# A graph layer with attention over 100,000 edges: earlier dst rows, two row tiles for the edge products, pieces of a second branch spread differently

## The reference, cut to what matters

```
xn  = layernorm(x)                                    # 6250 nodes x 256
q, k, v = xn @ Wq.T + bq, ...                         # 8 heads of 32
e   = edge_attr @ We.T                                # 100,000 edges, 64 -> 256
alpha = sum((q[dst]) * (k[src] + e)) / sqrt(32)       # per edge and head
w   = softmax of alpha over the edges of one dst
gnn = segment_sum((v[src] + e) * w, dst) + xn @ Wskip.T + bskip
mix = linear attention over all nodes, Wo, layernorm, relu FFN 256-1024-256, layernorm
x   = x + gnn + mix
out = x + mixture of 8 experts (three 256x256 layers each, all experts, softmax gates) of layernorm(x)
```

## Time and profile before

| | us |
|---|---|
| three runs | 3732.03, 3732.52, 3723.98 (median 3732.03) |
| profiled execution | 3703.33 |
| its span | 3701.4 |

### The profile page before, as it was taken

How to read it: one execution, slowest core, us unless ns; L and a number is a source line. 1 busy time by engine, 2 the same in 40 slices (tenths; PEclk the granted TensorE clock), 3 DMA queues, 4 the chain that set the end, 5 groups by cost and what they waited for, 6 DMA issues and landing times.

```text
span 3701.4 us, 72350 instructions
## 1 busy us (share of the span) xinstructions
PE 3241.8 (88%) x17312; PEld 2525.9 (68%) x17312; DVE 2927.2 (79%) x6394; ACT 1719.3 (46%) x4685; POOL 1259.3 (34%) x1313
## 2 busy tenths in 40 slices
PE   4998899999999899999999177777768999999999
PEld 3775566666666666666666145555558999999999
DVE  6776898898888888888888888888856666666665
ACT  1222333333333333333333156666646777777776
POOL 1223666666666666666664021111100000000000
PEclk9998999999999999999999599999979999999999
DMA  7336988898888988888888256666610000000000
GB/s 177 116 115 172 243 250 238 234 249 242 243 245 238 245 237 244 244 246 239 245 238 222 91 173 207 206 207 206 207 60 12 12 17 11 17 11 17 11 17 9
DMA packets 520911, 593.54 MB, mean 160 GB/s; under 512 B 187937, under 2 KB 396979, under 8 KB 520319
## 3 DMA queue, kind: packets, MB, share of 16 engines
q1 hardware_dynamic: 312408, 351.02, 32.7%
q0 software_dynamic: 201888, 232.77, 24.1%
q10 hardware_dynamic: 6409, 7.46, 0.6%
HBM read 426.91 MB, written 163.17 MB: 159 GB/s over the span
## 4 chain that ended last, share of the span: by engine, by line
PE 52%; DVE 18%; issue 13%; SPq 5%; DMA 3%; DVEq 3%; ACT 3%; ACTq 2%; another core or an unknown queue 0%
PE psum L635 10%; PE psum L637 10%; PE psum L636 10%; PE psum L713 6%; PE psum L697 5%; DMA region_s<-ab_d 3%; DVE weights L1373 3%; DVE part L1387 3%; PE psum L849 3%; PE psum L770 2%; DVE region_s L1572 2%; DVE region_x L1560 1%; ACTq L1088 1%; ACT region_s L1083 1%; DVEq L1563 1%
## 5 line engine op out<-in xcount | busy, mean ns | idle before, releaser
L600 POOL DMA_INDIRECT weights<-kv_tab,idx x450 | 547.7, 1217 | 351.9 <-ACT idx L1006 192.1
L1012 ACT ACTIVATE weights<-psum,region_s 125x250 f32<-125x250 f32 x450 | 211.7, 471 | 951.2 <-PE psum L713 524.6
L697 PE MATMUL psum<-we,weights 64*125 64x256 f32 x1800 | 578.4, 428 | 6.5 <-issue 3.4
L849 PE MATMUL psum<-region_s 125*125 125x264 f32 x1800 | 453.9, 401 | 128.8 <-DVE region_s L1572 128.8
L713 PE MATMUL psum<-region_x,weights 125*125 x1800 | 546.9, 429 | 0.0
L1129 ACT ACTIVATE region_s<-psum,bns 128x250 f32<-128x250 f32 x800 | 403.4, 555 | 287.2 <-PE psum L637 287.2
L1622 DVE TENSOR_TENSOR parts_h<-region_s,parts_h 128x500 fp32r<-128x500 f32 x400 | 269.9, 679 | 312.4 <-ACT parts_h L1133 283.1
L849 PEld LDWEIGHTS psum<-region_s 125*125 125x125 f32 x1800 | 304.6, 188 | 277.9 <-issue 152.7
L713 PEld LDWEIGHTS psum<-region_x,weights 125*125 125x125 f32 x1800 | 320.3, 198 | 190.2 <-issue 159.6
L600 POOL DMA_INDIRECT kv_more<-kv_tab,idx x300 | 364.2, 1214 | 142.6 <-issue 102.0
L697 PEld LDWEIGHTS psum<-we,weights 64*125 64x125 f32 x1800 | 291.2, 190 | 163.2 <-issue 148.0
(11 more groups left out here) (246 smaller groups left out, 7628.2 us busy)
## 6 DMA issues: line engine op xcount, KB each, us to landing
region_s<-ve_d SPq DMA_DIRECT2D x450, 256.0 KB, 2.9
ve_d<-weights SPq DMA_DIRECT2D x225, 256.0 KB
ve_d<-kv_more SPq DMA_DIRECT2D x150, 256.0 KB
weights<-in_attr_t SPq DMA_DIRECT2D x450, 62.5 KB
ve_d<-region_r SPq DMA_DIRECT2D x75, 256.0 KB
kv_tab<-region_s SPq DMA_DIRECT2D x50, 224.0 KB
region_s<-ab_d SPq DMA_DIRECT2D x450, 1.0 KB
weights<-kv_tab,idx POOLq DMA_INDIRECT x450
```

What stands on the lines that cost most here:

```text
L600: nc.gpsimd.indirect_dma_start(kg[r][0:T, w, :], None, kv_tab, bass.IndirectOffsetOnAxis(idx[:, r, w:w + 1], 0)).then_inc(gathered[r], 16)
L697: last = mm(psum[0:T, s % 2, w * D:(w + 1) * D], att_b[:, s % RP, w * T:(w + 1) * T], we[:, :], start=True, stop=True)
L849: last = mm(bank, hot[:, s, w, :], pv[:, s, w, 0:PV], start=(w == 0), stop=(w == 1))
```

## The change

The dst rows of a step are loaded three steps sooner, first thing in SP's step. The edge attributes of a pair go to 128 partitions (tile 0 in rows 0 to 63, tile 1 in rows 64 to 127, rows of 500 bytes), the weights `we` are loaded twice, and the two edge products of a step run one after the other on the two row halves, each into a bank of its own, 0 and 1; so product k waits for add k-1. `spread`'s operands move to rows 0 to 63, and it follows both products. The query product runs one step ahead of the edge product. The pieces of the branch get other steps, the last four products of `down` in the next block, and `up`'s banks change. DVE's register loads go behind the add, in D behind the first product. In D the one-hots of step 0 come from DVE, of 1, 3 and 5 from ACT, of 2 and 4 from POOL by two compares each.

```diff
+AHEAD = 3
...
-BY_DVE = {0: 1, 3: 2}
-BY_ACT = {1: 1, 2: 2, 4: 3, 5: 4}
+BY_DVE = {0: 1}
+BY_ACT = {1: 1, 3: 2, 5: 3}
+BY_POOL = {2: 1, 4: 2}
...
-we = sb("we", [ED, D])
+we = sb("we", [2 * ED, D])
...
-ab_b = carve(8200, RP * E2 // 2).bitcast(BF16).rearrange("p (r n) -> p r n", r=RP)[64:128]
-coef = weights[64:128, 1600:1600 + 64].bitcast(BF16)[:, 0:T]
+ab_b = carve(8200, RP * E2 // 2).bitcast(BF16).rearrange("p (r n) -> p r n", r=RP)[0:64]
+coef = weights[0:64, 1600:1600 + 64].bitcast(BF16)[:, 0:T]
...
-att_b = weights[0:ED, 0:RP * E2].rearrange("p (r t) -> p r t", r=RP)
+att_b = weights[:, 0:RP * T].rearrange("p (r t) -> p r t", r=RP)
...
-hot_dve, hot_act = sem("hot_dve"), sem("hot_act")
+hot_dve, hot_act, hot_pool = sem("hot_dve"), sem("hot_act"), sem("hot_pool")
...
-CONST_A, CONST_B = 16 * 7, 16 * 9
+CONST_A, CONST_B = 16 * 7, 16 * 10
...
-    sp.dma_start(we[:, :], a["w_e"]).then_inc(c_b, 16)
+    for w in range(2):
+        sp.dma_start(we[w * ED:(w + 1) * ED, :], a["w_e"]).then_inc(c_b, 16)
...
+    ab_regs = [sp.alloc_register(f"sp_ab{s}") for s in range(SU)]
     def load_ab(k, s, reg):
...
+    sp.load(ab_regs, walk[0:1, 0, 0:SU])
+    for s in range(AHEAD):
+        load_ab(s, s, ab_regs[s])
...
     def b_body(b, u):
...
+                sp.load(ab_regs, walk[0:1, 0, bass.ds(k + AHEAD, SU)])
+            if k + AHEAD < STEPS:
+                load_ab(k + AHEAD, (s + AHEAD) % SB, ab_regs[s % SU])
...
-            sp.dma_start(att_b[:, s % RP, :], a["attr_t"][:, bass.ds(i * E2, E2)]).then_inc(att_in[s % RP], 16)
-            load_ab(k, s, regs[s % SU])
+            sp.dma_start(att_b[:, s % RP, :], a["attr_t"][:, bass.ds(i * E2, E2)].rearrange("p (w t) -> w p t", w=2)).then_inc(att_in[s % RP], 16)
...
+    order = Order(pool, pool_o)
     def d_body(it):
-        for s in BY_ACT:
+        for s in range(SU):
+            if s in BY_DVE:
+                continue
...
-            nc.gpsimd.tensor_tensor(place_in[:, s, :], pv[:, s, :, D + H], jb_all[:, bass.ds(k, 1)].broadcast_to((T, 2)),
-                                    ALU.subtract).then_inc(place_ready, 1)
+            placed = nc.gpsimd.tensor_tensor(place_in[:, s, :], pv[:, s, :, D + H], jb_all[:, bass.ds(k, 1)].broadcast_to((T, 2)),
+                                             ALU.subtract)
+            if s in BY_ACT:
+                placed.then_inc(place_ready, 1)
+            else:
+                order(placed)
+                for w in range(2):
+                    compared = nc.gpsimd.tensor_scalar(hot[:, s, w, :], iota[:, :], place_in[:, s, w:w + 1], None, ALU.is_equal)
+                compared.then_inc(hot_pool, 1)
+        order.reset()
...
-    def eproj(k, s, turn_of, w):
-        if w == 0:
-            pe.wait_ge(att_in[s % RP], turn_of * 16)
-            wait(pe, kv_added, k - 1)
-        last = mm(psum[0:T, s % 2, w * D:(w + 1) * D], att_b[:, s % RP, w * T:(w + 1) * T], we[:, :], start=True, stop=True)
-        if w == 1:
-            last.then_inc(e_done, 1)
+    def eproj(k, s, turn_of):
+        pe.wait_ge(att_in[s % RP], turn_of * 16)
+        wait(pe, kv_added, k)
+        for w in range(2):
+            half = slice(w * ED, (w + 1) * ED)
+            last = mm(psum[0:T, w, 0:D], att_b[half, s % RP, :], we[half, :], start=True, stop=True)
+        last.then_inc(e_done, 1)
     def spread(k, s, turn_of):
...
-            if n == 4 and not (isinstance(b, int) and b == NB - 1):
-                pe.wait_ge(m_an, b + 2)
...
-                pe.wait_ge(m_hr, b * 4 + pair - 1)
+                pe.wait_ge(m_hr, b * 4 + pair)
...
-                last = mm(psum[:, 5 + pair % 2, o * BN:(o + 1) * BN], wm1[:, c, n * 128:(n + 1) * 128], mx1t[:, c, :],
+                last = mm(psum[:, 5 if pair == 0 else 6, o * BN:(o + 1) * BN], wm1[:, c, n * 128:(n + 1) * 128], mx1t[:, c, :],
...
-    mix_at = {2: ("q", 0), 3: ("q", 1), 7: ("attend",), 10: ("turn",), 11: ("out", 0), 12: ("out", 1)}
-    late_at = {1: ("turn1",), 3: ("up", 0), 4: ("up", 1), 5: ("up", 2), 6: ("up", 3), 10: ("up", 4), 11: ("up", 5),
-               12: ("up", 6), 13: ("up", 7), 14: ("down", 0, 3), 15: ("down", 3, 7), 16: ("down", 7, 11), 17: ("down", 11, 16)}
+    mix_at = {2: ("q", 0), 3: ("q", 1), 8: ("attend",), 11: ("turn",), 12: ("out", 0), 13: ("out", 1)}
+    late_at = {1: ("turn1",), 4: ("up", 0), 5: ("up", 1), 6: ("up", 2), 7: ("up", 3), 9: ("up", 4), 10: ("up", 5),
+               11: ("up", 6), 12: ("up", 7), 14: ("down", 0, 3), 15: ("down", 3, 6), 16: ("down", 6, 9), 17: ("down", 9, 12)}
+    last_at = {0: ("down", 12, 14), 1: ("down", 14, 16)}
     def b_body(b, u):
...
-                pe.load(regs, walk[0:1, 1, bass.ds(k, SU)])
-            some = s >= LAGQ or not (isinstance(b, int) and b == 0)
-            if some:
-                eproj(k - LAGQ, (s - LAGQ) % SB, b * (SB // RP) + (s - LAGQ) // RP + 1, 0)
+                pe.load(regs, walk[0:1, 1, bass.ds(k + 1, SU)])
+            if s >= LAGQ or not (isinstance(b, int) and b == 0):
+                eproj(k - LAGQ, (s - LAGQ) % SB, b * (SB // RP) + (s - LAGQ) // RP + 1)
...
-            if some:
-                eproj(k - LAGQ, (s - LAGQ) % SB, b * (SB // RP) + (s - LAGQ) // RP + 1, 1)
-                qprod(k - LAGQ, (s - LAGQ) % SB, regs[s % SU])
+            if s >= LAGQ - 1 or not (isinstance(b, int) and b == 0):
+                qprod(k - LAGQ + 1, (s - LAGQ + 1) % SB, regs[s % SU])
+            if s in last_at and not (isinstance(b, int) and b < 2):
+                mix(b - 2, u, last_at[s])
...
-    pe.load(regs, walk[0:1, 1, STEPS:STEPS + SU])
+    pe.load(regs, walk[0:1, 1, STEPS + 1:STEPS + 1 + SU])
...
-        eproj(STEPS - LAGQ + s, SB - LAGQ + s, (STEPS - LAGQ + s) // RP + 1, 0)
+        eproj(STEPS - LAGQ + s, SB - LAGQ + s, (STEPS - LAGQ + s) // RP + 1)
...
-        eproj(STEPS - LAGQ + s, SB - LAGQ + s, (STEPS - LAGQ + s) // RP + 1, 1)
-        qprod(STEPS - LAGQ + s, SB - LAGQ + s, regs[s])
-    for g in late_at.values():
+        if s < LAGQ - 1:
+            qprod(STEPS - LAGQ + 1 + s, SB - LAGQ + 1 + s, regs[s])
+        if s in last_at:
+            mix(NB - 2, 1, last_at[s])
+    for g in (*late_at.values(), *last_at.values()):
...
     def sums(k, s, it):
...
+        elif s in BY_POOL:
+            pe.wait_ge(hot_pool, it * len(BY_POOL) + BY_POOL[s])
...
-                last = fn(mh[:, n, :], psum[:, 5 + pair % 2, o * BN:(o + 1) * BN], ACT.Relu,
+                last = fn(mh[:, n, :], psum[:, 5 if pair == 0 else 6, o * BN:(o + 1) * BN], ACT.Relu,
...
-    mix_at, late_at = {1: "phi", 8: "turn", 17: "turn1"}, {2: 0, 4: 1, 9: 2, 11: 3}
+    mix_at, late_at = {1: "phi", 9: "turn", 17: "turn1"}, {3: 0, 5: 1, 8: 2, 10: 3}
     def b_body(b, u):
...
-        tt(rows4, rows4, psum[0:T, s % 2, :].rearrange("p (w d) -> p w d", w=2).unsqueeze(2).broadcast_to((T, 2, 2, D)),
+        tt(rows4, rows4, psum[0:T, 0:2, 0:D].unsqueeze(2).broadcast_to((T, 2, 2, D)),
...
     def multiply(k, s):
...
-    mix_at = {0: "phi", 3: "attend", 8: "sum1", 9: "stats1", 10: "root", 11: "root2", 12: "norm1", 13: "gain1"}
+    mix_at = {0: "phi", 4: "attend", 8: "sum1", 9: "stats1", 10: "root", 11: "root2", 12: "norm1", 13: "gain1"}
...
-    last_at = {1: "root2", 4: "norm2", 5: "gain2", 6: "add2"}
+    last_at = {1: "root2", 3: "norm2", 5: "gain2", 6: "add2"}
     def b_body(b, u):
...
-            if s % SU == 0:
-                dve.load(regs, walk[0:1, 2, bass.ds(k, SU)])
...
+            if s % SU == 0:
+                dve.load(regs, walk[0:1, 2, bass.ds(k, SU)])
...
     def d_body(it):
-        dve.load(regs, walk[0:1, 1, bass.ds(it * SU + LAGQ - LAG, SU)])
...
+            if s == 0:
+                dve.load(regs, walk[0:1, 1, bass.ds(it * SU + LAGQ - LAG, SU)])
```

## The result

| | us |
|---|---|
| before, beside it | 3732.28 (3723.98 to 3742.75) |
| after | 3815.53 (3809.42 to 3822.16, 4 runs) |
| ratio | 1.0222, 95% interval 1.0191 to 1.0253 |
| forecast | 3667, range 3580 to 3745 |

What follows compares the result with a forecast made beforehand. DVE was taken to bound both stages, with PE nearly full in the edge stage. Edge stage -16 us and segment sums -49 made -65, from the median 3732.0 to 3667 us, range 3580 to 3745.

Steps and rivals of the forecast that it cites:

- the one on SP: SP's queue: store and attribute load behind the earlier dst rows are needed over 15 us later; cost 0, bound +150.
- Register load behind the add: Edge stage: load hidden by the add at steps 0 and 6, outlasting it at step 12; -41 us (-79 to 0).
- `out` 1 too late: Edge stage: moved to PE step 13, `out` makes DVE wait before `sum1`, 2.5 us a block; +63 us (0 to +76).
- PE's waits: Edge stage: of some 60 us of DVE waits for PE and remote, 38 go and 22 stay; -38 us.
- Segment sums: Segment-sum stage: one one-hot leaving DVE -29, load moved -50, DVE delayed by POOL compares +30; -49 us together.
- the lock's +30: Segment-sum stage: POOL compares and DVE products block each other, 0.1 us a compare; +30 us, bounds 0 and +138.
- Row tiles overlap: Edge stage, PE: both edge products run side by side, 0.85 us to the first query pass, empty step 1.9 us.
- B: Rival, chance 0.13: low clock in PE steps 11 to 13 doubles DVE's wait for `out` in twelve blocks; 3780 us.
- A: Rival, chance 0.16: PE ahead everywhere, `out` in time, no wait for PE stays in the edge stage; -180, 3552 us.
- C: Rival, chance 0.05: in the segment sums all 300 compares block DVE whole; +138 instead of +30, 3775 us.
- D: Rival, chance 0.06: in the edge stage row tiles don't overlap, edge products stay in sequence; +13, 3680 us.
- listed as "right": Edge products starting together; 2.5 us idle a block before `sum1`; no dst-row wait; segment sums near 524 us; POOL compares stretched.

Runs made afterwards that it cites:

- e2: The changed kernel with each pair's attributes laid out as 128 plain DRAM rows, so the load is two-dimensional: 3569.1 us, ratio 0.9600.
- e9: e2 with DVE's edge-stage register load back at the head of steps 0, 6 and 12: 3645.9 us, ratio 0.9810.
- e7: e2 with `out` 1 a step earlier, at PE's step 12, and `up` 7 at 13: 3530.7 us, ratio 0.9493.
- e4: The kernel before with only the change's new segment sums: 3653.4 us, ratio 0.9825.
- e12: e2 with the branch tables of the kernel before: 3561.9 us, ratio 0.9565.
- e10: e7 without row tiles: edge products as before, in sequence, two banks by turns, query product in its own step: 3543.7 us, ratio 0.9545.
- e13: e2 with one unused DRAM row between the table's halves, making the load's outermost dimension 2 again: 3810.1 us, ratio 1.0240.
- e5: The changed kernel with the attribute load issued by ACT instead of SP, SP's register load for it removed: 3799.9 us, ratio 1.0227.

## Why the prediction was wrong

**The step that failed** is the one on SP: "Behind it on SP are the store of step k-6 and the attribute load of step k [...] Both are needed five steps, over 15 us, later: cost 0." It asked when the load is due and never what the load has become. The load's new shape, 128 partitions with the two tiles outermost, has no term in the sum and is in no rival; the bound of +150 was for SP's register load. The runs put +231 us there (ratio 1.0222 of after less 0.9600 of e2, times 3721). Being early didn't help, since the transfers were not late once but too slow in each step, 4.1 us against the 3.6 us of e2. A ring of six covers a delay, never a rate.

**The rest of the sum** held in direction, and came to -149 us (e2) where -65 was forecast: -77 for the register load, -67 for the segment sums and some -5 for all other terms together:

- *Register load behind the add*, -41: too small. It is -77 (e9 less e2). The direct part is near the forecast: I let 1.5 us stay at each step 12 and nothing at steps 0 and 6, 38 us in all. In e2 the idle time between add and multiply, beyond the 0.04 us of every step, is 22 us in the whole stage, 14 of them at step 12 (0.6 us each) and 8 at steps 0 and 6. The row of the multiply (e2, then e9, 400 to 1900 us) shows the difference:

```profile
L1405 DVE TENSOR_TENSOR weights<-weights,psum 125x512 f32<-125x512 f32 x210 | 144.2, 687 | 28.1 <-DVE weights L1397 17.3 <-issue 4.4
```
```profile
L1405 DVE TENSOR_TENSOR weights<-weights,psum 125x512 f32<-125x512 f32 x201 | 138.0, 686 | 6.9
```

The "issue" ahead of the pieces in e9, 63.3 us in 1500, is 71 in 25 blocks. 71 less 22 is 49. The other 28 us lie elsewhere (DVE waits 9.3 us for PE's edge product in e9, which is not among e2's waits, and PE's clock is 0.96 instead of 0.98); what links them to the load is not shown.

- *`out` 1 too late*, +63: right in place and mechanism. Forecast 2.5 us in each of 25 blocks; measured 53.5 us in 23 waits (2.3 each, e2), of which e7 gave back 38 in the time.
- *PE's waits*, -38: together with `out` the sum was +25. The pair that shows it is e9 and e4, which share the new segment sums and the register loads as before: e9 is 6 us below e4 by the ratios (0.9810 and 0.9825), with intervals that overlap almost wholly. With +38 for `out` and -9 for the dst rows some -35 are left, near the forecast, but known to tens of us only. The single terms inside are bracketed: levelling about 30 us (e12 against e7), row tiles 13 to 19 (e10).
- *Dst rows*, 0: about -9.
- *Segment sums*, -49: they are -67, and e4 alone gives -67.5 in the time (its new sums in 505 us), so they depend on nothing else. From stretches inside the stage (469.93 of 550 us busy before, 451.88 of 490 from 2330 to 2820 us after) DVE's busy time fell by 23 us and its idle time by 44, where one-hot and load had -29 and -50 ("issue" before L1584 is now 36.0 where the loops' head had 84.0). At most 12 us are left for the lock's +30, the term that was mis-sized. POOL's compares were stretched, as forecast: 0.94 us in the median against 0.59 in the shortest (I had taken 0.46). DVE's product stayed at 0.684 against 0.687 us; 37 of 449 took over 0.70. No run takes the products away from the compares, so that POOL waits for them is an inference.

```profile
L636 POOL TENSOR_SCALAR region_s<-iota,region_s x300: 591/938/1314, 2318.8 to 2822.8; 125x125 f32<-125x125 f32 x150
...
DVE region_x L1584 <- issue: 36.0, 68, 0.9
```

- *Row tiles overlap*, as said: four edge passes and the spread, 0.82 us in the median from the first edge pass to the first query pass (forecast 0.85), 0.73 in the step shown. In order of time, after:

```profile
1055.67 0.70 PE L719 MATMUL psum<-we,weights 64*125 64x256 f32 x4
1056.20 0.27 PE L726 MATMUL psum<-region_s,weights 64*125 64x250 bf16 x1
1056.40 1.13 PE L734 MATMUL psum<-region_x,weights 125*125 x4
```

**The rivals.** The time came out 36 us above B (3780), and not by B's mechanism. The low clock (0.92 in the edge stage) follows from the slow transfers: e13 has 0.93 and e2 0.98 with the same work on PE. With the load laid flat the time is near A's (3569 in e2; A, given 0.16, has 3552), but that nearness is luck: A had `out` arrive in time, and e2 still waits 53.5 us for it. C and D didn't happen. Two signs listed as "wrong" came: blocks of 74.1 us (1847.5 / 449 x 18) and a clock under 0.94. All that were listed as "right" came too, the segment sums shorter than the 524 us given there, so the list had no sign for a slow load.

## What to carry to other kernels

When a DMA gets another shape, cost its rate, not only its due time: which of its dimensions is outermost, how many packets fly at once, and what share of the step that leaves on the engines that carry it. A load for two partition halves should be one run of 128 partitions, or, 38 us dearer here, two DMAs, but not `w p t` with w = 2. A mean DMA share that falls while everything waits, and a long issue of a transfer that isn't at fault, are how such a load looked in this profile. When it is gone, undo the other parts one by one in the mended kernel: only there did their worth show.

## What was not expected of the hardware

- The load with outermost dimension 2 slows the DMA issued behind it on SP's queue: the 1 KB dst rows' issue went from 0.25 to 1.08 us (1.13 in e13), with maxima of 5.6 and 6.2 us, while the attribute load's own issue stayed at 0.55 us (0.50 before). A reader who trusts the longest instruction looks at the wrong line.
- With that load on ACT's queue, SP's issue recovered (0.24 us) and the time didn't. There the next DMA behind the load is mostly the next such load, and its own issue took 1.00 us in the median, 7.9 at most (e5). So the slow issue goes where the load goes, and SP's queue isn't what is short.
- Beside POOL's 300 compares DVE's product has about the same median as before (0.684 against 0.687 us, longest 0.801 against 0.695): POOL's compares are stretched by over half, DVE's products hardly.
- The register load of six values takes about as long behind the add as ahead of the branch (1.74 us median in e2, 1.89 in e9), and moving it was worth 77 us, more than levelling (about 30) and row tiles (13 to 19) together.
